# Splitting the second expert layer of a two-layer sparse block into three groups of tokens (4, 2 and 2 steps) instead of two (4 and 4)

## The chip, the cores and the metric

One Trainium2 chip, and of it one core. The metric is the device time of one execution in microseconds (us); lower is better. All data is float32, except where a routing count is made with bf16 ones and zeros. Engine names are those of the profile: PE is TensorE, DVE is VectorE, ACT is ScalarE, POOL is GpSimd, and SP is SyncE, which only issues DMAs here.

## The reference, cut to what matters

The input is x with shape (4, 1024, 128). Three residual sub-layers follow each other: an expert layer, an attention layer, and the same expert layer again with the same weights.

```python
def ffn(x):                       # x: (4, 1024, 128); 8 experts, hidden width 512
    xf = x.reshape(-1, 128)
    e = argmax(xf @ Wr.T + br)    # one expert for each token
    h = relu(xf @ W1[e].T + b1[e])
    return h @ W2[e].T + b2[e]    # the reference computes all 8 and picks one
x = x + 0.5 * ffn(layernorm(x))
x = x + attention(layernorm(x))   # linear attention, 16 heads, chunks of 128 tokens, with decay and a gate
x = x + 0.5 * ffn(layernorm(x))
```

## The kernel before

**Units, slots and tiles.** The 1024 positions of each of the 4 sequences are cut into 8 steps of 128, so a step holds 4 tiles of 128 tokens, one for each sequence. An expert layer does not run over steps. It sorts the tokens by expert and runs over slots, each of 128 places that all belong to one expert. A unit is a group of steps that are sorted together. For a unit of t tiles, t + 7 slots are always run, because each of the 8 experts can end in a slot that is not full. `SPLIT = ((3, 5), (4, 4))` makes two units in each layer: 12 tiles and 19 slots, 20 tiles and 27 slots in layer one; twice 16 tiles and 23 slots in layer two. Slots are numbered through by G: 0 to 45 are layer one, 46 to 68 are unit 2, and 69 to 91 are unit 3. In this text y(G) stands for the DVE instruction at line 820 that finishes slot G.

**What happens for a unit.** DVE takes the best expert of each token from the router's logits (`route_choose`), PE adds up the counts (`route_counts`), and DVE works out each token's place (`route_read_counts`, `route_count`, `route_place`) and the expert that owns each slot (`route_owners`). Then POOL sends each tile of 128 rows (576 bytes a row) to its places in a DRAM buffer `slots_in` by an indirect DMA, one for each tile (`sort_rows`, line 384). SP loads slots from there into a ring of 24 places in SBUF (`load_slot`, line 315) and the expert's W1 into a ring of 4 (`load_w1`, line 323).

**One slot.** DVE normalises the rows (line 798). PE transposes them (line 1034), ACT copies the result out of PSUM (line 499), PE does 8 matmuls with W1 (line 1042), ACT and DVE each take half of the relu (lines 514 and 813), PE does 8 matmuls with W2 (line 1052), and DVE adds the result to the row (line 820). That makes 17 matmul records for each slot. The slots are pipelined: in the loop's turn G, PE transposes slot G + 1, does the first product of G and the second of G - 1. POOL then scatters the finished rows to x1 or to the output by an indirect DMA, one for each slot (`scatter`, line 395). W1, b1 and b2 are addressed through registers that each engine loads from the owners' row.

**Order around the change.** Each engine's program is in order. Work of the attention layer's end and the routing of the last unit lie between the slots of layer two; a table `between` in each engine's `expert_pass(1, ...)` names the turn of each piece. POOL's order for layer two is: sort unit 2 in the attention layer's last part, scatter slots 46 to 51 (`EARLY_SCATTERS = 6`), sort unit 3, scatter all others. Before each scatter, and before each row sort of a unit that is not the first in its layer, POOL clears a piece of SBUF (`pause`, line 371), which puts a space between indirect DMAs. SP issues in its turn G the load of slot G + 6 and the W1 of slot G + 3. The load of a unit's first slot waits until the whole unit is sorted, and a load into a used ring place waits for the scatter of slot G - 24. POOL also takes a part of DVE's sums in the attention layer (`half_sum`, line 433); that is the same in both kernels.

Of the kernel before, what the change touches and what calls it, by code (L numbers as in the profile page):

```python
# [17 lines left out]
STEPS = SEQ // P  # L18
# [3 lines left out]

SPLIT = ((3, 5), (4, 4))
LAYERS, GROUPS = len(SPLIT), 2
UNITS = LAYERS * GROUPS
Unit = namedtuple("Unit", "layer first tiles slots start")
# [14 lines left out]
UNIT = list_units()  # L41
LAYER_TILES = UNIT[GROUPS].start
MAX_TILES = max(u.tiles for u in UNIT)
# [36 lines left out]
def step(k):  # L80
    return Step(k, k % 2)
# [20 lines left out]
def build(nc, x, w1t, bias, w2t, wrt, br, wqkv, wg1t, wg2, wo, gamma, beta, decay, const, out):  # L102
    with ExitStack() as ctx:
        def sb(name, shape, dt=F32):
            return ctx.enter_context(nc.sbuf_tensor(name, shape, dt))
# [73 lines left out]

        owner_ff = sb("owner_ff", [1, LAYER_TILES], I32)  # L180
        owner_d = sb("owner_d", [1, LAYER_TILES], I32)
        owner_fb = sb("owner_fb", [1, LAYER_TILES], I32)
        slot_of = [sb(f"slot_of{u}", [P, UNIT[u].tiles], I32) for u in range(UNITS)]

# [68 lines left out]
        ln_turn = lambda k: max(k + 1, 0)  # L253
        EARLY_SCATTERS = 6
        ROUTE_TURN = SPLIT[1][0] - 1 + 3

# [6 lines left out]
        wait_scattered = lambda eng, G: eng.wait_ge(scattered[G % SCATTER_SEMS], 16 * (G // SCATTER_SEMS + 1))  # L263
        layer_of = lambda G: G // LAYER_TILES
        unit_of = lambda G: max(u for u in range(UNITS) if UNIT[u].start <= G)
# [17 lines left out]
        def _(sp):  # L283
# [24 lines left out]
            def load_slot(G):  # L308
                u = unit_of(G)
                if first_of_unit(G):  # L310
                    sp.wait_ge(rows_sorted[u], 16 * UNIT[u].tiles)
                if G >= RING:
                    wait_scattered(sp, G - RING)
                at = (G - UNIT[u].start) * P
                sp.dma_start(in_ring(G), slots_in[u][at:at + P, :]).then_inc(slot_loaded[G % LOAD_SEMS], 16)

            def load_w1(G):
                if first_of_unit(G):
                    sp.wait_ge(owners_known[unit_of(G)], 1)
                k = G % LAYER_TILES  # L320
                e = sp.value_load(owner_ff[0:1, k:k + 1], min_val=0, max_val=(EXPERTS - 1) * FF)
                wait(sp, up_b, G - W1_BUFS + 1)
                sp.dma_start(w1_ring[G % W1_BUFS][:, :], w1t[:, bass.ds(e, FF)]).then_inc(w1_loaded[G % W1_BUFS], 16)
# [4 lines left out]
            SLOTS_AHEAD, W1_AHEAD, X1_AT = 6, 3, 36  # L328

            def loads(first, end, hooks):  # L330
                for G in range(first - SLOTS_AHEAD, end):
                    if G in hooks:
                        hooks[G]()
                    if G + SLOTS_AHEAD < end:
                        load_slot(G + SLOTS_AHEAD)
                    if first <= G + W1_AHEAD < end:
                        load_w1(G + W1_AHEAD)
# [6 lines left out]

            loads(0, LAYER_TILES, {X1_AT: first_group_back})
            for G in range(UNIT[1].start, LAYER_TILES):
                wait_scattered(sp, G)
            for c in range(SPLIT[0][0], STEPS):
                load_x1(c)
            fill_slots(2)  # L350
            fill_slots(3)
            loads(LAYER_TILES, LAYERS * LAYER_TILES, {})
            for G in range(LAYERS * LAYER_TILES - SCATTER_SEMS, LAYERS * LAYER_TILES):
                wait_scattered(sp, G)
# [3 lines left out]
        def _(pool):  # L358
# [15 lines left out]
            def sort_rows(u):  # L374
                unit = UNIT[u]
                pool.wait_ge(rows_kept, unit.layer * STEPS + (unit.first + unit.tiles) // BATCH)
                pool.wait_ge(fill_ready, 4)
                pool.wait_ge(ids_ready, 1 + 2 * min(u + 1, GROUPS))
                pool.wait_ge(slots_known[u], 1)
                pool.wait_ge(slots_filled[u], 16)  # L380
                for t in range(unit.tiles):
                    if u % GROUPS == 1:
                        pause()
                    pool.indirect_dma_start(  # L384
                        slots_in[u], bass.IndirectOffsetOnAxis(ap=slot_of[u][:, t:t + 1], axis=0),
                        row_of(unit.first + t), None).then_inc(rows_sorted[u], 16)
# [73 lines left out]
            sort_rows(1)  # L460
            scatter(0, LAYER_TILES)
            for b in range(BATCH):
# [3 lines left out]
            sort_rows(2)  # L466
            scatter(LAYER_TILES, LAYER_TILES + EARLY_SCATTERS)
            sort_rows(3)
            scatter(LAYER_TILES + EARLY_SCATTERS, LAYERS * LAYER_TILES)


        @block.scalar
        def _(act):
# [19 lines left out]
            def expert_pass(l, between):  # L493
                base, end = l * LAYER_TILES, (l + 1) * LAYER_TILES

# [137 lines left out]
            for k in TURNS:  # L633
# [3 lines left out]
                3: lambda: output_copy(8), 4: lambda: normalise_routed(8),  # L637
                6: lambda: route_copy(STEPS + 6, 0, bank[4]), 9: lambda: normalise_routed(9),
                11: lambda: route_copy(STEPS + 7, 1, bank[4])})


        @block.vector
        def _(dve):
# [130 lines left out]
            def route_owners(u):  # L774
                chain, slots = chains[u], UNIT[u].slots
                at = UNIT[u].start % LAYER_TILES
                part, owner_ = slice(at, at + slots), owner_f[:, 0:slots]
# [14 lines left out]
            def expert_pass(l, between):  # L792
                base, end = l * LAYER_TILES, (l + 1) * LAYER_TILES

# [179 lines left out]
            for k in TURNS:  # L974
# [5 lines left out]
                0: lambda: (output_stats(8), residual_stats(8), turn_small(8, 0, SMALL + 1, *both)),  # L980
                2: lambda: router_bias(5), 4: lambda: gate(step(7)), 5: lambda: residual_stats(9),
                6: lambda: (turn_small(9, 0, 6, ROUTED, ROUTED + BATCH), router_bias(6)),
                7: lambda: turn_small(9, 6, SMALL + 1, ROUTED, ROUTED + BATCH),
                11: lambda: (router_bias(7), route_choose(3)), 12: lambda: (route_read_counts(3), route_count(3)),
                13: lambda: route_place(3), 14: lambda: route_owners(3)})


        @block.tensor
        def _(pe):
# [32 lines left out]
            def expert_pass(l, between):  # L1022
                base, end = l * LAYER_TILES, (l + 1) * LAYER_TILES
                expert = {}
# [58 lines left out]
            def gate_product(s):  # L1083
                if s.n == 0:
                    pe.wait_ge(y_done, LAYER_TILES)
                wait(pe, delta_copied, s.n)
                mm(bank[6][:, :], wg_sb[:, :], xnT[s.par][:, :], start=True, stop=True).then_inc(gate_ready, 1)
# [116 lines left out]
            for k in TURNS:  # L1204
# [11 lines left out]
                2: lambda: out_transpose(step(7)), 4: lambda: (out_product(step(7)), route_transpose(step(6))),  # L1216
                5: lambda: route(6), 9: lambda: route_transpose(step(7)), 10: lambda: route(7),
                11: lambda: route_counts(3)})

# [61 lines left out]
```

## Time and profile before

| what | value |
|---|---|
| three runs | 505.95, 510.1 and 514.2 us; median 510.1 us |
| the profiled execution's own time | 506.26 us |
| its span, first to last instruction | 504.5 us |
| lies outside the span | 1.76 us |
| mean granted PE clock | 0.86 of full speed |
| y(46), the first slot of layer two finished | 366.40 us |
| y(91), the last slot finished | 497.02 us |

The span is the stretch that the trace covers, and positions in it are in us from its start. The runs lie within 1.6% of each other.

### The profile page before, as it was taken

How to read it: one execution, taken by the hardware profiler on the slowest of the kernel's cores; microseconds unless marked ns; L12 is line 12 of the kernel's file. 1: busy time of each engine (PE TensorE's matmuls, PEld its weight loads, DVE VectorE, ACT ScalarE, POOL GpSimd, SP SyncE). 2: the span in 40 equal slices, each digit the busy share in tenths (PEclk: the TensorE clock that was granted, in tenths of full speed). 3: DMA queues.
4: the chain of work that ended last, by engine and by line, in shares of the span. 5: the costliest groups of instructions: out<-in, count | busy, mean ns of one | idle time of the engine just before them, and what ended most of it. 6: DMA issues, size and time to landing. Idle time of an engine off the chain costs nothing.

```text
span 504.5 us, 10554 instructions
## 1 busy us (share of the span) xinstructions
PE 375.3 (74%) x2474; PEld 328.9 (65%) x2474; DVE 349.1 (69%) x1064; ACT 192.9 (38%) x590; POOL 302.4 (60%) x402
## 2 busy tenths in 40 slices
PE   4593049999999677976878869382699773499983
PEld 2592049999998456655656657362698563399983
DVE  3937006878777169999999999996777721167861
ACT  1360014555554413253562744402465211145541
POOL 1057885666665526778577676957051388856564
PEclk9655558999999879999999999677799975589998
DMA  8972425666674290000000000011554422356730
GB/s 246 282 308 83 147 80 153 196 200 199 200 238 125 67 298 15 0 2 0 2 1 1 0 1 1 0 36 59 157 155 144 119 75 78 106 149 195 206 116 6
DMA packets 54218, 56.08 MB, mean 111 GB/s; under 512 B 6828, under 2 KB 39881, under 8 KB 53904
## 3 DMA queue, kind: packets, MB, share of 16 engines
q1 hardware_dynamic: 48736, 45.85, 31.4%
q0 software_dynamic: 4992, 8.94, 4.9%
q10 hardware_dynamic: 432, 0.63, 0.4%
q8 instruction: 23, 0.38, 0.3%
q14 instruction: 35, 0.29, 0.2%
HBM read 39.69 MB, written 17.53 MB: 113 GB/s over the span
## 4 chain that ended last, share of the span: by engine, by line
PE 30%; DVE 22%; issue 20%; POOL 15%; another core or an unknown queue 6%; ACT 3%; DMA 1%; DVEq 1%; POOLq 1%; ACTq 0%
PE bank L1052 9%; PE bank L1042 8%; POOL out_x L395 7%; PE bank L1100 4%; POOL scratch L371 3%; DVE o_in L859 3%; POOL slots_in L384 3%; DVE st L646 2%; PE bank L1080 2%; PE bank L1006 2%; PE bank L1012 2%; PE bank L1134 2%; DVE tt L670 1%; DVE qS L850 1%
## 5 line engine op out<-in xcount | busy, mean ns | idle before, releaser
L1042 PE MATMUL bank<-slot_xT,w_ring 128*128 128x128 f32 x736 | 107.7, 290 | 20.1 <-issue 12.7
L1042 PEld LDWEIGHTS bank<-slot_xT,w_ring 128*128 128x128 f32 x736 | 96.3, 202 | 25.0 <-issue 20.8
L813 DVE TENSOR_SCALAR hT_b<-bank,b_cur 128x128 f32<-128x128 f32 x184 | 55.7, 344 | 49.8 <-remote 44.8
L384 POOL DMA_INDIRECT slots_in<-rows,slot_of x64 | 61.9, 967 | 47.1 <-DVE slot_of L772 32.8
L371 POOL MEMSET scratch<- 128x256 f32 x128 | 40.9, 320 | 64.8 <-DVE ring L820 35.5
L1100 PE MATMUL bank<-outer_all,decay_sb 128*128 128x256 f32 x256 | 70.5, 402 | 7.2 <-DVE outer_all L276 2.7
L1052 PE MATMUL bank<-w_sb,hT_a 128*128 x368 | 63.5, 298 | 12.4 <-issue 6.9
L514 ACT ACTIVATE hT_a<-bank,b_cur 128x128 f32<-128x128 f32 x184 | 57.3, 363 | 33.2 <-remote 18.1
L1100 PEld LDWEIGHTS bank<-outer_all,decay_sb 128*128 128x128 f32 x256 | 49.5, 203 | 24.4 <-issue 6.7
L276 POOL TENSOR_TENSOR outer_all<-qkv 128x512 f32<-128x512 f32 x60 | 63.6, 1084 | 2.6 <-ACT qkv L542 2.4
L1052 PEld LDWEIGHTS bank<-w_sb,hT_a 128*128 128x128 f32 x368 | 51.4, 202 | 17.2 <-issue 16.5
L1052 PE MATMUL bank<-w_sb,hT_b 128*128 x368 | 58.9, 285 | 0.0
L395 POOL DMA_INDIRECT x<-ring x46 | 44.6, 970 | 19.1 <-POOL scratch L371 18.7
L395 POOL DMA_INDIRECT out_x<-ring x46 | 44.9, 975 | 18.0 <-POOL scratch L371 13.7
L859 DVE TENSOR_REDUCE o_in<-qS 128x64 f32<-128x256 f32 (+1 forms) x64 | 53.5, 856 | 0.0
L820 DVE SCALAR_TENSOR_TENSOR ring<-bank,ring 128x128 f32<-128x128 f32 x92 | 26.7, 290 | 37.2 <-issue 14.2
L1052 PEld LDWEIGHTS bank<-w_sb,hT_b 128*128 128x128 f32 x368 | 51.4, 202 | 0.0
L850 DVE TENSOR_TENSOR qS<-bank,qkv 128x512 f32<-128x512 f32 x64 | 43.4, 679 | 11.5 <-PE bank L1100 7.2
L433 POOL TENSOR_TENSOR qS<-qS 128x256 f32<-128x256 f32 x28 | 20.3, 727 | 43.9 <-DVE qS L850 43.9
L507 ACT ACTIVATE b_cur<-b_t 128x4 f32 x92 | 18.9, 205 | 72.0 <-DVE hT_b L813 47.2
L798 DVE TENSOR_SCALAR slot_n<-ring 128x128 f32<-128x128 f32 x92 | 45.3, 494 | 1.2 <-DMA ring<-slots_in 0.9
L499 ACT ACTIVATE slot_xT<-bank 128x128 f32<-128x128 f32 x92 | 25.1, 273 | 46.9 <-remote 31.5
(117 smaller groups left out, 559.0 us busy)
## 6 DMA issues: line engine op xcount, KB each, us to landing
w_ring<-in_w1t SPq DMA_DIRECT2D x92, 256.0 KB
ring<-slots_in SPq DMA_DIRECT2D x92, 72.0 KB
slots_in<-fill SPq DMA_DIRECT2D x2, 1656.0 KB, 13.1
rows<-in_x SPq DMA_DIRECT2D x8, 256.0 KB, 6.4
w_sb<-in_w2t SPq DMA_DIRECT2D x1, 2048.0 KB
rows<-x SPq DMA_DIRECT2D x8, 256.0 KB, 5.0
slots_in<-fill SPq DMA_DIRECT2D x1, 1944.0 KB, 15.0
slots_in<-fill SPq DMA_DIRECT2D x1, 1368.0 KB, 8.7
```

Of the source, the lines that this page charges most:

```text
L276: return eng.tensor_tensor(u_.rearrange("p (h d e) -> p h d e", d=HD, e=HD), k_.rearrange("p (h d) e -> p h d e", d=HD), v_, ALU.mult)
L371: pool.memset(scratch[k % 2][:, :], 0.0).then_inc(paused, 1)
L384: pool.indirect_dma_start(slots_in[u], bass.IndirectOffsetOnAxis(ap=slot_of[u][:, t:t + 1], axis=0), row_of(unit.first + t), None).then_in ...
L395: pool.indirect_dma_start(x1 if layer_of(G) == 0 else out, bass.IndirectOffsetOnAxis(ap=ids_in_ring(G), axis=0), in_ring(G, 0, D), None, b ...
L514: last = nc.scalar.activation(hT_a[G % 2][:, f * P:(f + 1) * P], bank_a[:, f * P:(f + 1) * P], ACT.Relu, bias=b1_cur[G % 2][:, f:f + 1])
L798: nc.vector.tensor_scalar(slot_n[G % 3][:, :], in_ring(G, 0, D), in_ring(G, SCALE_AT, SCALE_AT + 1), in_ring(G, SHIFT_AT, SHIFT_AT + 1), A ...
L813: last = nc.vector.tensor_scalar(hT_b[G % 2][:, f * P:(f + 1) * P], bank_b[:, f * P:(f + 1) * P], b1_cur[G % 2][:, 2 + f:3 + f], 0.0, ALU. ...
L850: nc.vector.tensor_tensor(qS[h % 4][:, :].rearrange("p (b a e) -> p b a e", b=BATCH, e=HD), bank[h % 3][:, :].rearrange("p (b a e) -> p b ...
L859: nc.vector.tensor_reduce(o_in[:, h * w:(h + 1) * w].rearrange("p (a e) -> p a e", e=HD), qS[h % 4][:, :].rearrange("p (a d e) -> p a e d" ...
L1042: last = mm(to[:, f * P:(f + 1) * P], w1_ring[G % W1_BUFS][:, (2 * half + f) * P:(2 * half + f + 1) * P], slot_xT[G % 2][:, :], start=True ...
L1052: last = mm(y_bank[:, 0:D], h[:, f % 2 * P:(f % 2 + 1) * P], w2_sb[:, bass.ds(expert[G] + f * D, D)], start=(f == 0), stop=(f == FB - 1))
L1100: last = mm(to, decay_sb[:, (2 * h + a) * P:(2 * h + a + 1) * P], u, start=True, stop=True)
```

## The change

Layer two is sorted in three groups of 4, 2 and 2 steps. Unit 3 now has 8 tiles and 15 slots (69 to 83) and unit 4 has 8 tiles and 15 slots (84 to 98). POOL's order becomes: sort unit 2, 6 scatters, sort unit 3 (8 tiles), 18 scatters (52 to 69), sort unit 4 (8 tiles), the other scatters. The routing of unit 3 moves from turns 11 to 14 of the pass to turns 2 to 7; that of unit 4 lies in turns 13 to 17. The load of the first slots of a later unit is put off to 3 turns ahead of the unit instead of 6. Layer one and the attention code are as before.

```diff
-SPLIT = ((3, 5), (4, 4))
-LAYERS, GROUPS = len(SPLIT), 2
-UNITS = LAYERS * GROUPS
+SPLIT = ((3, 5), (4, 2, 2))
+LAYERS, GROUPS = len(SPLIT), len(SPLIT[0])
+UNITS = sum(len(s) for s in SPLIT)
...
-        EARLY_SCATTERS = 6
+        EARLY_SCATTERS = (6, 24)
...
+            def slot_due(H):
+
+                u = UNIT[unit_of(H)]
+                return H - SLOTS_AHEAD if u.first == 0 else max(H - SLOTS_AHEAD, u.start - W1_AHEAD)
...
-                    if G + SLOTS_AHEAD < end:
-                        load_slot(G + SLOTS_AHEAD)
+                    for H in range(first, end):
+                        if slot_due(H) == G:
+                            load_slot(H)
...
-            fill_slots(2)
-            fill_slots(3)
+            for u in range(GROUPS, UNITS):
+                fill_slots(u)
...
-                    if u % GROUPS == 1:
+                    if UNIT[u].first > 0:
                         pause()
...
             sort_rows(2)
-            scatter(LAYER_TILES, LAYER_TILES + EARLY_SCATTERS)
+            scatter(LAYER_START[1], LAYER_START[1] + EARLY_SCATTERS[0])
             sort_rows(3)
-            scatter(LAYER_TILES + EARLY_SCATTERS, LAYERS * LAYER_TILES)
+            scatter(LAYER_START[1] + EARLY_SCATTERS[0], LAYER_START[1] + EARLY_SCATTERS[1])
+            sort_rows(4)
+            scatter(LAYER_START[1] + EARLY_SCATTERS[1], LAYER_START[2])
...
-                6: lambda: route_copy(STEPS + 6, 0, bank[4]), 9: lambda: normalise_routed(9),
-                11: lambda: route_copy(STEPS + 7, 1, bank[4])})
+                6: lambda: route_copy(STEPS + 6, 0, bank[4]), 11: lambda: normalise_routed(9),
+                13: lambda: route_copy(STEPS + 7, 1, bank[4])})
...
-                2: lambda: router_bias(5), 4: lambda: gate(step(7)), 5: lambda: residual_stats(9),
-                6: lambda: (turn_small(9, 0, 6, ROUTED, ROUTED + BATCH), router_bias(6)),
-                7: lambda: turn_small(9, 6, SMALL + 1, ROUTED, ROUTED + BATCH),
-                11: lambda: (router_bias(7), route_choose(3)), 12: lambda: (route_read_counts(3), route_count(3)),
-                13: lambda: route_place(3), 14: lambda: route_owners(3)})
+                2: lambda: (router_bias(5), route_choose(3)), 4: lambda: (gate(step(7)), route_read_counts(3), route_count(3)),
+                5: lambda: residual_stats(9), 6: lambda: route_place(3),
+                7: lambda: route_owners(3), 8: lambda: (turn_small(9, 0, 6, ROUTED, ROUTED + BATCH), router_bias(6)),
+                9: lambda: turn_small(9, 6, SMALL + 1, ROUTED, ROUTED + BATCH),
+                13: lambda: (router_bias(7), route_choose(4)), 15: lambda: (route_read_counts(4), route_count(4)),
+                16: lambda: route_place(4), 17: lambda: route_owners(4)})
...
-                5: lambda: route(6), 9: lambda: route_transpose(step(7)), 10: lambda: route(7),
-                11: lambda: route_counts(3)})
+                5: lambda: route(6), 11: lambda: route_transpose(step(7)), 12: lambda: route(7),
+                3: lambda: route_counts(3), 14: lambda: route_counts(4)})
```

The other lines of the diff replace `LAYER_TILES` by the starts of the layers, since the two layers now have different numbers of slots (46 and 53).

## Rows read from the trace of the kernel before

**Rows 1.** The page, part 1: busy us (share of the span) xinstructions.
```profile
PE 375.3 (74%) x2474; PEld 328.9 (65%) x2474; DVE 349.1 (69%) x1064; ACT 192.9 (38%) x590; POOL 302.4 (60%) x402
```

**Rows 2.** The chain that ended last, 330 to 505 us, its shares by line.
```profile
by line: issue 22.0%; POOL out_x L395 20.9%; another core or an unknown queue 12.0%; POOL scratch L371 10.1%; POOL slots_in L384 8.8%; PE bank L1052 3.9%; PE bank L1042 3.4%; PE bank L1134 1.7%; DVEq L804 1.5%; DVE hT_b L813 1.0%; POOLq L86
```

**Rows 3.** Busy time by stretch in layer two; columns named in its first line.
```profile
core 0: us, PE busy (x) PEld busy (x) DVE busy (x) ACT busy (x) POOL busy (x), PEclk, DMA share, GB/s
...
399.00:412.00 13.00, 9.15 (x54) 7.83 (x54) 6.12 (x24) 3.08 (x13) 11.30 (x18) 0.85 0.32 103
412.00:423.00 11.00, 6.79 (x30) 5.41 (x29) 2.37 (x8) 1.38 (x5) 9.68 (x17) 0.66 0.14 50
423.00:433.00 10.00, 2.56 (x9) 1.85 (x8) 0.61 (x2) 0.83 (x3) 8.96 (x14) 0.50 0.48 143
...
463.00:479.00 16.00, 16.00 (x144) 15.97 (x143) 12.78 (x44) 9.35 (x34) 9.53 (x15) 1.00 0.72 209
```

**Rows 4.** Timeline of DVE, line 820: start, us, and idle before; y(55), y(58) to y(64).
```profile
388.33 0.29 DVE L820 SCALAR_TENSOR_TENSOR ring<-bank,ring 128x128 f32<-128x128 f32 x1 [0.28 <-PE bank L1052]
...
399.86 0.28 DVE L820 SCALAR_TENSOR_TENSOR ring<-bank,ring 128x128 f32<-128x128 f32 x1
...
402.71 0.28 DVE L820 SCALAR_TENSOR_TENSOR ring<-bank,ring 128x128 f32<-128x128 f32 x1
...
407.71 0.29 DVE L820 SCALAR_TENSOR_TENSOR ring<-bank,ring 128x128 f32<-128x128 f32 x1 [1.65 <-remote]
...
412.20 0.29 DVE L820 SCALAR_TENSOR_TENSOR ring<-bank,ring 128x128 f32<-128x128 f32 x1 [0.94 <-remote]
...
420.30 0.29 DVE L820 SCALAR_TENSOR_TENSOR ring<-bank,ring 128x128 f32<-128x128 f32 x1 [2.36 <-remote]
...
433.47 0.29 DVE L820 SCALAR_TENSOR_TENSOR ring<-bank,ring 128x128 f32<-128x128 f32 x1 [5.26 <-remote]
...
440.81 0.29 DVE L820 SCALAR_TENSOR_TENSOR ring<-bank,ring 128x128 f32<-128x128 f32 x1 [0.92 <-remote]
```

**Rows 5.** The same timeline later: y(66) and y(91).
```profile
446.51 0.29 DVE L820 SCALAR_TENSOR_TENSOR ring<-bank,ring 128x128 f32<-128x128 f32 x1 [0.44 <-PE bank L1052]
...
497.02 0.29 DVE L820 SCALAR_TENSOR_TENSOR ring<-bank,ring 128x128 f32<-128x128 f32 x1 [1.43 <-PE bank L1052]
```

**Rows 6.** Timeline of POOL: scatter(51), unit 3's first and last sort, scatter(63).
```profile
379.94 0.97 POOL L395 DMA_INDIRECT out_x<-ring  x1 [0.43 <-issue]
398.86 0.31 POOL L371 MEMSET scratch<- 128x256 f32 x1 [17.95 <-DVE slot_of L772]
399.54 0.97 POOL L384 DMA_INDIRECT slots_in<-rows,slot_of  x1 [0.38 <-issue]
...
421.40 0.96 POOL L384 DMA_INDIRECT slots_in<-rows,slot_of  x1 [0.17 <-issue]
...
438.97 0.97 POOL L395 DMA_INDIRECT out_x<-ring  x1 [0.17 <-issue]
```

**Rows 7.** Timeline of SP: W1 of slots 62 and 65, then slot 69.
```profile
393.65 0.34 SPq L323 DMA_DIRECT2D w_ring<-in_w1t  x1
...
405.56 0.34 SPq L323 DMA_DIRECT2D w_ring<-in_w1t  x1
423.71 0.32 SPq L315 DMA_DIRECT2D ring<-slots_in  x1
```

**Rows 8.** Timeline of layer one's start: slot 0 transposed by PE and copied by ACT.
```profile
48.37 0.47 PE L1034 MATMUL bank<-const_sb,slot_n 128*128 128x128 f32 x1 [0.35 <-issue]
...
65.64 0.28 ACT L499 ACTIVATE slot_xT<-bank 128x128 f32<-128x128 f32 x1 [20.88 <-remote]
```

**Rows 9.** Busy time by stretch while unit 2 is sorted (332.2 to 352.1 us).
```profile
332.00:344.00 12.00, 9.30 (x43) 7.05 (x41) 11.90 (x37) 1.09 (x2) 9.08 (x10) 0.96 0.16 56
344.00:350.00 6.00, 0.00 (x0) 0.00 (x0) 1.66 (x4) 0.00 (x0) 4.47 (x6) 0.72 0.15 51
```

**Rows 10.** Timeline of DVE: a routing operation on 128 and a small one on 4 elements.
```profile
379.84 0.16 DVE L677 SCALAR_TENSOR_TENSOR uu<-tt,var 128x4 f32<-128x4 f32 x1
...
390.44 0.29 DVE L739 TENSOR_REDUCE best<-place 128x16 f32<-128x128 f32 x1
```

More of the change, by code:

```diff
@@ L41 @@
 UNIT = list_units()
-LAYER_TILES = UNIT[GROUPS].start
+LAYER_START = [next(u.start for u in UNIT if u.layer == l) for l in range(LAYERS)] + [UNIT[-1].start + UNIT[-1].slots]
+LAYER_SLOTS = max(b - a for a, b in zip(LAYER_START, LAYER_START[1:]))
 MAX_TILES = max(u.tiles for u in UNIT)
@@ L177, in build @@
         owner_f = sb("owner_f", [1, MAX_SLOTS])
-        owner_ff = sb("owner_ff", [1, LAYER_TILES], I32)
-        owner_d = sb("owner_d", [1, LAYER_TILES], I32)
-        owner_fb = sb("owner_fb", [1, LAYER_TILES], I32)
+        owner_ff = sb("owner_ff", [1, LAYER_SLOTS], I32)
+        owner_d = sb("owner_d", [1, LAYER_SLOTS], I32)
+        owner_fb = sb("owner_fb", [1, LAYER_SLOTS], I32)
         slot_of = [sb(f"slot_of{u}", [P, UNIT[u].tiles], I32) for u in range(UNITS)]
@@ L263, in build @@
         wait_scattered = lambda eng, G: eng.wait_ge(scattered[G % SCATTER_SEMS], 16 * (G // SCATTER_SEMS + 1))
-        layer_of = lambda G: G // LAYER_TILES
+        layer_of = lambda G: max(l for l in range(LAYERS) if LAYER_START[l] <= G)
         unit_of = lambda G: max(u for u in range(UNITS) if UNIT[u].start <= G)
@@ L319, in load_w1 @@
                     sp.wait_ge(owners_known[unit_of(G)], 1)
-                k = G % LAYER_TILES
+                k = G - LAYER_START[layer_of(G)]
                 e = sp.value_load(owner_ff[0:1, k:k + 1], min_val=0, max_val=(EXPERTS - 1) * FF)
@@ L343, in first_group_back @@
                     load_x1(c)
-            loads(0, LAYER_TILES, {X1_AT: first_group_back})
-            for G in range(UNIT[1].start, LAYER_TILES):
+            loads(0, LAYER_START[1], {X1_AT: first_group_back})
+            for G in range(UNIT[1].start, LAYER_START[1]):
                 wait_scattered(sp, G)
@@ L349, in _ @@
                 load_x1(c)
-            fill_slots(2)
-            fill_slots(3)
-            loads(LAYER_TILES, LAYERS * LAYER_TILES, {})
-            for G in range(LAYERS * LAYER_TILES - SCATTER_SEMS, LAYERS * LAYER_TILES):
+            for u in range(GROUPS, UNITS):
+                fill_slots(u)
+            loads(LAYER_START[1], LAYER_START[2], {})
+            for G in range(LAYER_START[2] - SCATTER_SEMS, LAYER_START[2]):
                 wait_scattered(sp, G)
@@ L460, in _ @@
             sort_rows(1)
-            scatter(0, LAYER_TILES)
+            scatter(0, LAYER_START[1])
             for b in range(BATCH):
@@ L493, in expert_pass @@
             def expert_pass(l, between):
-                base, end = l * LAYER_TILES, (l + 1) * LAYER_TILES
+                base, end = LAYER_START[l], LAYER_START[l + 1]
                 def copy_xT(G):
@@ L775, in route_owners @@
                 chain, slots = chains[u], UNIT[u].slots
-                at = UNIT[u].start % LAYER_TILES
+                at = UNIT[u].start - LAYER_START[UNIT[u].layer]
                 part, owner_ = slice(at, at + slots), owner_f[:, 0:slots]
@@ L792, in expert_pass @@
             def expert_pass(l, between):
-                base, end = l * LAYER_TILES, (l + 1) * LAYER_TILES
+                base, end = LAYER_START[l], LAYER_START[l + 1]
                 def normalise_slot(G):
@@ L1022, in expert_pass @@
             def expert_pass(l, between):
-                base, end = l * LAYER_TILES, (l + 1) * LAYER_TILES
+                base, end = LAYER_START[l], LAYER_START[l + 1]
                 expert = {}
@@ L1084, in gate_product @@
                 if s.n == 0:
-                    pe.wait_ge(y_done, LAYER_TILES)
+                    pe.wait_ge(y_done, LAYER_START[1])
                 wait(pe, delta_copied, s.n)
```

## The prediction, made before the changed kernel was run

> **What bounds the kernel now.** The page's first part gives no engine more than 74% of the span [rows 1], so no engine's speed sets the whole, and the stage of the change has to be read by itself. The chain of waits for the last 175 us leads through POOL: scatters 20.9%, the clears before them 10.1%, row sorts 8.8% [rows 2]. A chain that runs along an engine that is merely busy beside the others proves little, so I went on to the busy times by stretch. From 463 to 479 us PE is busy for all of 16.00 us, with 144 matmul records [rows 3]. At 17 a slot that is 8.5 slots, or 1.9 us a slot: this is the free pace, and PE sets it. From 399 to 433 us every engine but POOL is mostly idle: PE is busy 9.15 of 13, 6.79 of 11 and then 2.56 of 10 us, and its granted clock falls to 0.85, 0.66 and 0.50, half speed, after it had thinned out [rows 3]. That is the hole in layer two.
>
> Its size: y(58) comes at 399.86 and y(66) at 446.51 [rows 4, 5], 8 slots in 46.65 us where 8 x 1.9 = 15.2 would do, so 31.4 us are lost. POOL's timeline runs over the same stretch: idle for 17.95 us until unit 3's places are known, then 16 sorts from 399.54 to 421.40 (15 spacings, 1.46 us each), and without a gap 12 late scatters, slots 52 to 63, to 438.97 [rows 6]. I call such a run of 28 indirect DMAs at 1.46 us a dense spell. y(64) comes only 1.84 us after the last of them [rows 4, 6], and the pace is back at once. In the spell the slots come later and later: the intervals from y(58) to y(64) are 2.85, 5.0, 4.5, 8.1, 13.2 and 7.3 us [rows 4].
>
> There are two readings. One: dense POOL DMAs hold up the signals between the other engines. Two: SP's queue is blocked, since it waits at slot 69's load from 405.56 to 423.71 for the sort, with W1 of slot 66 behind it [rows 7]. For the second, the times agree roughly. Against it: W1 of slot 62 was issued at 393.65 and that of slot 65 at 405.56 [rows 7], yet y(62) came at 420.30 and y(63) at 433.47 [rows 4], with nothing of theirs in the blocked queue. For the first, layer one has a purer case: under 20 sorts PE began slot 0's transpose at 48.37 (0.47 us), and ACT, which had only to copy it, began at 65.64 [rows 8], 17 us later. I take the first.
>
> **The change part by part.** The sum is made on the profiled execution, 504.5 us of span and 1.76 outside it, 506.26 in all; that is 3.8 us below the median of 510.1. I add the same difference to the median.
>
> *Seven more slots.* Layer two has 53 slots instead of 46, whatever the data: 7 x 1.9 = 13.3 us, all on PE's path [rows 3]. Nothing covers them; each also needs a W1 load and a scatter, which fit beside 1.9 us as they do for the others.
>
> *Routing twice.* Now `route_choose`, the counts and `route_place` lie in three turns, y(55) to y(58): 11.53 us for 3 slots [rows 4], 5.8 over pace. (The owners' turn falls into the spell and is counted there.) The new units have 64 wide elements instead of 128. An operation takes 0.29 us at 128 and 0.16 at 4 [rows 10], so some 0.22 at 64 (between them on a line); some 14 wide operations in a routing save 1.0 us. Two routings cost 2 x 4.85 = 9.7: 3.9 more. They stand in DVE's order ahead of the relu, so nothing hides them.
>
> *The long spell goes:* -31.4 us.
>
> *Two short spells come.* POOL no longer idles before the sort, because unit 3's places are known by turn 6, when scatter(51) goes out. The sort is 8 x 1.46 = 11.7 us. I lay the slots over it as they came in the old spell, which has the same start: at +1.0, +3.9, +8.9 and +13.3 us from the sort's start [rows 4, 6]. So three scatters are late when it ends, the fourth falls due while they are sent, and the spell ends after 12 DMAs, 17.5 us. The next slot then comes at about +19 instead of at +21.4. That makes 4 slots in 18.0 us against 7.6: 10.4 us. The second sort, after scatter(69), finds the same: 20.8 in all. Bounds: from below nothing, since while unit 2 was sorted DVE was busy for 11.90 of the first 12 us with 10 sorts issued; from above a standstill, as in the 6 us after them, where PE did nothing [rows 9], and in layer one [rows 8]. In a standstill hardly any scatter falls late: 10 DMAs, 14.6 us, and 1.9 us for the two slow slots after it (y(64) to y(66), 5.7 us against 3.8 [rows 4, 5]), so 33 us for both. I take 20.8 because the old spell lies in the same loop with the same loads, and its first third is exactly this piece.
>
> *Moves with one answer, at nothing.* The scatters of the old order are kept, and POOL's queue has no idle of its own while slots wait. `route_counts(3)` in PE's turn 3 waits for DVE's turn 2, but the product behind it needs that turn's relu anyway. The fill of a third buffer (7 slots x 72 KB more) is issued long before, behind the attention layer. A gain below nothing is possible for SP: its wait moves behind W1 of slot 68, and the sort is over by then (about 395 us). In its place comes a shorter lead: the first load of a unit is issued when PE is through with slot 64 (79), and DVE wants it some 2.5 turns later, 4.7 us; as a row for such a load there is only the general pace. From nothing to 5 us for both units; I take nothing, as the ring's other loads are never waited for at pace.
>
> Sum: 13.3 + 3.9 - 31.4 + 20.8 = +6.6. Span 511.1, own time 512.9; on the median 510.1 + 6.6 = 516.7 us.
>
> **The rivals.** *Standstill:* each short spell stops everything, as in layer one. 13.3 + 3.9 - 31.4 + 33 = +18.8: 529 us, slower. It decides from 12.3 us a spell on, where the whole passes 2%. For it: layer one's 17 us [rows 8], and W1 loads run all through the new spells, while from 405.56 to 423.71 SP issued none [rows 7]; the two worst intervals came with and after the loads' return. Against it: the old spell's own first 12 us.
>
> *Short spells are nearly covered:* signals grow late only with the spell's length, 12 us are free as for unit 2 [rows 9], and each costs one late hand-over or two, 3 us. 17.2 - 31.4 + 6 = -8.2: 502 us. Against it: y(60) was 3 us late within 9 us [rows 4].
>
> *It was SP's queue:* the hole came from the blocked loads, the new order waits nowhere, and dense spells are free. 17.2 - 31.4 = -14.2: 496 us, faster. The rows against it stand above. The Trainium skill speaks for this case: "SBUF — State Buffer", section "Who interferes with whom", says that only the port pair that VectorE and GpSimd share causes contention, and that "PE and ACT never wait on anyone". By that rule POOL's sorts could not hold PE or ACT, and the change would come out at this rival's 496 us. The trace speaks against it, if the 17 us between PE's end and ACT's start in layer one [rows 8] are no port's matter but a late signal, which the page does not treat.
>
> *Late first loads* at the two unit borders, 5 us on top of the forecast: 522 us.
>
> **How the numbers follow.** A measurement of this kernel can tell about 2% from no change, that is 10.2 us: below 499.9 is faster, above 520.3 slower. The forecast's own case, 512 to 522 us, has 0.47; the standstill 0.25; covered spells 0.14; SP's queue 0.09; late loads 0.05. Faster is SP's queue with a share of the covered case, 0.12. Slower is the standstill without its mildest form, the late loads and the top of the forecast's case, 0.36. Within 2% remains, 0.52. The range reaches over the covered case and to the standstill, 501 to 529, and leaves out SP's queue and the worst of the standstill.
>
> **What would show it.** In the new profile: y(46) to the last y should take 137 us (130.6 before), with 53 of them; two spells of some 12 indirect DMAs at 1.46 us, from about 383 us and some 45 us later; in each 4 slots take 16 to 20 us, and PE's clock dips briefly or not at all; three turns over pace in each routing, 4.85 us; free pace 1.9 us. If a spell has fewer than 3 slots, the standstill holds; if it has 6 or more, one of the two fast rivals. The sum is wrong if the late signals depend on something other than the spell, such as loads that run beside it, since I scaled by length alone; and it is wrong in the other direction if late signals of the first spell last into the paced part, where POOL sends a DMA every 1.9 us.

## The result, and the profile after

The changed kernel takes 520.83 us in the median of 4 runs (519.99 to 522.66), the kernel before 508.02 in 4. The ratio is 1.0267, with a 95% interval from 1.0216 to 1.0318: slower by 12.8 us, just beyond the 2% that the prediction treats as no change. Here and below a median is over all executions of a kernel, while a ratio leaves out the few executions that were disturbed as a whole, so it is not exactly the quotient of two medians. The profiled execution has a span of 518.2 us and a time of 519.99.

The page, part 1, of the changed kernel, which answers to [rows 1]:

```profile
PE 392.1 (76%) x2595; PEld 345.4 (67%) x2595; DVE 363.2 (70%) x1124; ACT 200.8 (39%) x618; POOL 311.2 (60%) x416
```

PE has 121 records more: 7 slots of 17 are 119. The chain of waits from 340 us on leads through POOL again. The stretch isn't the one of [rows 2], which begins at 330 us, but the shares of POOL's scatters and sorts are clearly larger now:

```profile
by line: issue 39.7%; POOL out_x L403 27.3%; POOL slots_in L392 14.7%; POOL scratch L379 12.0%; POOLq L88 1.2%; POOLq L403 0.8%; POOLq L105 0.7%; POOLq L388 0.0%; POOLq L387 0.0%
```

The timeline of DVE, line 830 (line 820 of before), shows the slots: y(46), y(52) to y(56), then y(70) to y(75), and y(98). It answers to [rows 4, 5].

```profile
368.67 0.29 DVE L830 SCALAR_TENSOR_TENSOR ring<-bank,ring 128x128 f32<-128x128 f32 x1 [0.69 <-PE bank L1063]
...
387.47 0.28 DVE L830 SCALAR_TENSOR_TENSOR ring<-bank,ring 128x128 f32<-128x128 f32 x1
...
393.89 0.29 DVE L830 SCALAR_TENSOR_TENSOR ring<-bank,ring 128x128 f32<-128x128 f32 x1 [2.40 <-remote]
...
399.88 0.29 DVE L830 SCALAR_TENSOR_TENSOR ring<-bank,ring 128x128 f32<-128x128 f32 x1 [1.65 <-remote]
...
403.67 0.29 DVE L830 SCALAR_TENSOR_TENSOR ring<-bank,ring 128x128 f32<-128x128 f32 x1 [0.19 <-remote]
...
407.37 0.29 DVE L830 SCALAR_TENSOR_TENSOR ring<-bank,ring 128x128 f32<-128x128 f32 x1 [1.10 <-PE bank L1063]
...
441.16 0.29 DVE L830 SCALAR_TENSOR_TENSOR ring<-bank,ring 128x128 f32<-128x128 f32 x1 [0.24 <-issue]
...
446.09 0.29 DVE L830 SCALAR_TENSOR_TENSOR ring<-bank,ring 128x128 f32<-128x128 f32 x1 [3.19 <-remote]
...
452.10 0.29 DVE L830 SCALAR_TENSOR_TENSOR ring<-bank,ring 128x128 f32<-128x128 f32 x1 [2.40 <-remote]
...
458.78 0.29 DVE L830 SCALAR_TENSOR_TENSOR ring<-bank,ring 128x128 f32<-128x128 f32 x1 [1.65 <-remote]
...
461.42 0.29 DVE L830 SCALAR_TENSOR_TENSOR ring<-bank,ring 128x128 f32<-128x128 f32 x1 [1.00 <-PE bank L1063]
...
464.02 0.29 DVE L830 SCALAR_TENSOR_TENSOR ring<-bank,ring 128x128 f32<-128x128 f32 x1 [0.28 <-PE bank L1063]
...
510.18 0.29 DVE L830 SCALAR_TENSOR_TENSOR ring<-bank,ring 128x128 f32<-128x128 f32 x1 [1.43 <-PE bank L1063]
```

Layer two, from the first finished slot to the last, takes 141.5 us; before it took 130.6 [rows 5, and the table of the times]. In place of one hole there are two, 19.9 us for 4 slots and 20.3 us for 4. In both, DVE waits for something whose sender the trace doesn't name ("remote"). What y(53) needed from PE was the second product of slot 53, and PE had ended it at 389.62 us:

```profile
388.47 0.71 PE L1063 MATMUL bank<-w_sb,hT_a 128*128 x4
...
389.01 0.61 PE L1063 MATMUL bank<-w_sb,hT_b 128*128 x4
```

DVE was free from 391.49 us on, and yet y(53) began only at 393.89. This is what "a late signal" means below: the work is done, and the engine that waits for it starts some microseconds later. POOL's timeline (line 392 is a sort, 403 a scatter) has the sorts of unit 3 from 387.22 to 397.41 and of unit 4 from 442.39 on, each after a scatter and at 1.46 us. Three late scatters follow each group of 8 sorts at the same spacing, to 401.81 and 456.99, so a spell is 11 indirect DMAs. These rows answer to [rows 6]:

```profile
385.76 0.97 POOL L403 DMA_INDIRECT out_x<-ring  x1 [0.43 <-POOL scratch L379]
386.73 0.33 POOL L379 MEMSET scratch<- 128x256 f32 x1
387.22 0.96 POOL L392 DMA_INDIRECT slots_in<-rows,slot_of  x1 [0.17 <-issue]
...
397.41 0.96 POOL L392 DMA_INDIRECT slots_in<-rows,slot_of  x1 [0.17 <-POOL scratch L379]
...
401.81 0.97 POOL L403 DMA_INDIRECT out_x<-ring  x1 [0.17 <-issue]
...
442.39 0.96 POOL L392 DMA_INDIRECT slots_in<-rows,slot_of  x1 [0.17 <-issue]
```

The busy times of the two holes answer to [rows 3]. Each PEclk is a mean over its stretch, so 0.72 and 0.65 hide that the clock is at its lower level, half speed, for a part of it. The third row is of a view of its own, cut to such a part, and shows 0.50.

```profile
392.00:398.00 6.00, 3.39 (x16) 2.91 (x14) 2.10 (x11) 0.90 (x3) 5.34 (x9) 0.72 0.33 104
...
447.00:454.00 7.00, 4.29 (x22) 3.80 (x22) 1.67 (x6) 1.57 (x7) 6.21 (x10) 0.65 0.29 92
...
401.60:407.60 6.00, 4.35 (x21) 4.05 (x20) 2.48 (x9) 3.31 (x13) 2.30 (x4) 0.50 0.39 112
```

Read in this way, PE runs at half speed in four parts of the two holes (around 396, 404, 452 and 461 us), each after it had thinned out; in the kernel before it is at 0.50 from 408.5 to 414.5 and from 418.8 to 445.3 us. PE is still at 0.50 from 459.6 to 462.2 us, when POOL no longer sends at 1.46 us, and the two slots around it, y(74) and y(75), take 2.6 us each in place of 1.9. A spell's cost below includes such slots.

### The profile page after: what moved, and what is told of

Read it like the earlier page. It is cut to its first block, busy times and chain, and to the rows that moved or that the text cites. A ratio compares the mean times of both kernels' runs of the same rounds, so it can differ in the third digit from the quotient of the medians.

```text
span 518.2 us, 11134 instructions
## 1 busy us (share of the span) xinstructions
PE 392.1 (76%) x2595; PEld 345.4 (67%) x2595; DVE 363.2 (70%) x1124; ACT 200.8 (39%) x618; POOL 311.2 (60%) x416
## 4 chain that ended last, share of the span: by engine, by line
issue 27%; PE 22%; POOL 19%; DVE 17%; another core or an unknown queue 5%; SPq 4%; ACT 1%; POOLq 1%; DVEq 1%; DMA 0%; ACTq 0%
POOL out_x L403 9%; PE bank L1063 8%; PE bank L1053 7%; POOL slots_in L392 6%; POOL scratch L379 4%; DVE o_in L869 4%; PE bank L1111 3%; PE bank L1145 2%; PE bank L1091 2%; SPq L289 1%; SPq L299 1%; DVE qS L860 1%; DVE st L656 1%; DVE tt L680 1%
## 5 line engine op out<-in xcount | busy, mean ns | idle before, releaser
L1053 PE MATMUL bank<-slot_xT,w_ring 128*128 128x128 f32 x792 | 116.2, 289 | 17.6 <-DVE hT_b L823 8.2
L1053 PEld LDWEIGHTS bank<-slot_xT,w_ring 128*128 128x128 f32 x792 | 104.3, 203 | 22.6 <-issue 11.8
L823 DVE TENSOR_SCALAR hT_b<-bank,b_cur 128x128 f32<-128x128 f32 x198 | 59.9, 344 | 41.1 <-remote 35.4
L1063 PE MATMUL bank<-w_sb,hT_a 128*128 x396 | 67.1, 294 | 13.1 <-issue 7.9
L524 ACT ACTIVATE hT_a<-bank,b_cur 128x128 f32<-128x128 f32 x198 | 61.7, 363 | 27.6 <-PE bank L1053 16.4
L1063 PEld LDWEIGHTS bank<-w_sb,hT_a 128*128 128x128 f32 x396 | 54.4, 199 | 18.0 <-issue 17.6
L403 POOL DMA_INDIRECT out_x<-ring x53 | 51.5, 972 | 23.2 <-POOL scratch L379 20.0
L1063 PE MATMUL bank<-w_sb,hT_b 128*128 x396 | 63.2, 284 | 0.0
L1063 PEld LDWEIGHTS bank<-w_sb,hT_b 128*128 128x128 f32 x396 | 54.9, 201 | 0.0
L517 ACT ACTIVATE b_cur<-b_t 128x4 f32 x99 | 20.3, 205 | 82.5 <-DVE hT_b L823 65.8
L808 DVE TENSOR_SCALAR slot_n<-ring 128x128 f32<-128x128 f32 x99 | 50.2, 508 | 0.7 <-DMA ring<-slots_in 0.6
L441 POOL TENSOR_TENSOR qS<-qS 128x256 f32<-128x256 f32 x28 | 20.4, 728 | 46.4 <-DVE qS L860 46.4
L509 ACT ACTIVATE slot_xT<-bank 128x128 f32<-128x128 f32 x99 | 27.0, 273 | 44.8 <-remote 24.9
## 6 DMA issues: line engine op xcount, KB each, us to landing
slots_in<-fill SPq DMA_DIRECT2D x2, 1080.0 KB, 12.7
```

The costliest lines, as they stand in the source:

```text
L403: pool.indirect_dma_start(x1 if layer_of(G) == 0 else out, bass.IndirectOffsetOnAxis(ap=ids_in_ring(G), axis=0), in_ring(G, 0, D), None, b ...
L524: last = nc.scalar.activation(hT_a[G % 2][:, f * P:(f + 1) * P], bank_a[:, f * P:(f + 1) * P], ACT.Relu, bias=b1_cur[G % 2][:, f:f + 1])
L808: nc.vector.tensor_scalar(slot_n[G % 3][:, :], in_ring(G, 0, D), in_ring(G, SCALE_AT, SCALE_AT + 1), in_ring(G, SHIFT_AT, SHIFT_AT + 1), A ...
L823: last = nc.vector.tensor_scalar(hT_b[G % 2][:, f * P:(f + 1) * P], bank_b[:, f * P:(f + 1) * P], b1_cur[G % 2][:, 2 + f:3 + f], 0.0, ALU. ...
L1053: last = mm(to[:, f * P:(f + 1) * P], w1_ring[G % W1_BUFS][:, (2 * half + f) * P:(2 * half + f + 1) * P], slot_xT[G % 2][:, :], start=True ...
L1063: last = mm(y_bank[:, 0:D], h[:, f % 2 * P:(f % 2 + 1) * P], w2_sb[:, bass.ds(expert[G] + f * D, D)], start=(f == 0), stop=(f == FB - 1))
```

## The experiments

"Layer two" below is the time from y(46) to the last y in the profiled execution; it is free of the scatter of what lies ahead of it: y(46) came anywhere from 364.2 to 369.2 us in the 14 profiled executions, changed and unchanged alike. Ratios are to the kernel before, run on the same chip.

**Is it SP's blocked queue?** The kernel before with SP's order of the changed kernel alone:

```diff
-                    if G + SLOTS_AHEAD < end:
-                        load_slot(G + SLOTS_AHEAD)
+                    for H in range(first, end):
+                        if G == (max(H - SLOTS_AHEAD, UNIT[3].start - W1_AHEAD) if H >= UNIT[3].start else H - SLOTS_AHEAD):
+                            load_slot(H)
```

> The kernel before (groups of 4 and 4), with one edit of SP's order: the loads of unit 3's first slots are put off from 6 to 3 turns ahead, as in the changed kernel, so that W1 of slots 66 to 68 no longer stands behind the wait for the sort. Theory (dense POOL DMAs make the other engines' signals late): nothing changes, within 3 us of before, and the intervals from y(58) to y(64) stay at 3 to 13 us. Rival (the hole is SP's blocked queue): 25 to 31 us faster, and the hole is gone.

Measured: 504.55 us, ratio 0.9992 (0.9946 to 1.0038): no change. Its profiled execution took 510.17 us, so only its pattern is read: from y(59) on, the seven slots to y(66) came at 5.2 to 6.6 us each. The blocked queue was not what limited the kernel before. But the pattern did change: without it the intervals no longer grow to 13.2 us. It will come back below.

**Is it POOL's order?** `EARLY_SCATTERS = 13` instead of 6 in the kernel before.

> The kernel before, with EARLY_SCATTERS 13 in place of 6: POOL scatters slots 52 to 58 while it waits for unit 3's places, and sorts then. Theory: 7 late scatters leave the spell, which becomes 16 sorts and about 5 scatters, 21 DMAs and 31 us instead of 28 and 41; the loss of 31 us shrinks to about 24, so 7 us faster (3 to 12). Rival (only the sort itself, or SP's wait for its end, counts): the sort starts and ends at the same time, so no change.

Measured: 497.07 us, ratio 0.9846 (0.9761 to 0.9931), layer two 121.2 us. A one-number edit makes the kernel before faster, by 0.7 to 2.4%, and so is better than both kernels; whether it passes 2% is open. The late scatters count, not only the sorts.

**What do the spells cost in all?** Both kernels without their later sorts:

```diff
-                if first_of_unit(G):
+                if first_of_unit(G) and u <= 2:
                     sp.wait_ge(rows_sorted[u], 16 * UNIT[u].tiles)
...
-                sp.dma_start(in_ring(G), slots_in[u][at:at + P, :])
+                sp.dma_start(in_ring(G), slots_in[min(u, 2)][at:at + P, :])
...
             def sort_rows(u):
+                if u > 2:
+                    return
```

> The kernel before without the 16 row sorts of unit 3: its slots are loaded from unit 2's sorted rows, so the output lacks unit 3's tokens, while all loads, products and scatters stay. It measures what the long spell costs in all. Theory and rival alike: about 31 us faster than before. If it is under 20, the hole has another cause than the sorts and what follows them.

> The changed kernel (4, 2 and 2) without the row sorts of units 3 and 4, whose slots are loaded from unit 2's sorted rows; the output lacks their tokens. The change without its spells: theory says 25 us faster than the changed kernel (the two spells cost 12.5 us each by its trace), which is 12 us faster than before and 17 to 19 us slower than the kernel before without its sorts (7 slots at 1.9 us and a second routing). If the difference between the two kernels without sorts is far from 17, the slots or the routing were mis-sized and not the spells.

Measured: 480.52 us (ratio 0.9528, 0.9462 to 0.9594) and 493.67 us (ratio 0.9778, 0.9659 to 0.9897). Layer two takes 99.5 us without sorts in groups of 4 and 4, and 116.6 in groups of 4, 2 and 2. So the spells cost 130.6 - 99.5 = 31.1 us before and 141.5 - 116.6 = 24.9 after, and slots and routing 17.1 us. The whole of the first kernel gained only 24.5, less than layer two did: its last 11.2 us behind y(91), against 7.5 before, took 3.7 of it back, and y(46) came 1.5 us later. For the same reasons the two kernels without sorts differ by only 13.2 us as wholes, where 17 to 19 was expected; the 17.1 us are layer two's alone.

**Is it POOL's time or its DMAs?** In the kernel without sorts, each sort of units 3 and 4 becomes two more clears:

```diff
                     if UNIT[u].first > 0:
                         pause()
+                    if u > 2:
+                        pause()
+                        pause()
+                        continue
```

> The changed kernel without the row sorts of units 3 and 4 (their slots are loaded from unit 2's sorted rows, the output lacks their tokens), but with POOL kept busy in each sort's place by two more clears, some 1.5 us a tile. It parts POOL's time from its DMAs. Theory (indirect DMAs in close order make the other engines' signals late): as without sorts, 120 to 123 us from y(46) to the last y against 116.6 without sorts and 141.5 in the changed kernel, the rest for the late scatters sent in close order; the whole at 494 to 500 us. Rival (what counts is that POOL is busy and scatters fall late): as the changed kernel, 520 us.

Measured: 505.29 us, ratio 0.9969 (0.9918 to 1.0020), layer two 130.4 us. Neither expectation was met, and the trace says why. The 24 clears took 6.4 us, where 8 sorts take 11.7, so they matched the sorts' time on POOL only in part. Its timeline, 24 clears and that of the next scatter in one run on POOL:

```profile
383.74 6.41 POOL L379 MEMSET scratch<- 128x256 f32 x25
```

and DVE (line 812 is the normalising of a slot) and PE beside it:

```profile
384.69 5.54 DVE L812 TENSOR_SCALAR slot_n<-ring 128x128 f32<-128x128 f32 x1
...
385.49 0.71 PE L1067 MATMUL bank<-w_sb,hT_a 128*128 x4
...
386.03 0.61 PE L1067 MATMUL bank<-w_sb,hT_b 128*128 x4
...
390.29 0.48 PE L1049 MATMUL bank<-const_sb,slot_n 128*128 128x128 f32 x1 [3.64 <-DVE slot_n L812]
```

One DVE instruction that takes 0.34 to 0.54 us elsewhere takes 5.54, as long as the clears follow each other, and PE then waits for it by name. The second run of clears holds the same instruction for 6.44 us. These two stops (8.1 us for y(53) where the kernel without sorts takes 3.1, 8.5 for y(72) where it takes 1.9) are 11.6 of the 13.8 us over the kernel without sorts. It is another stop than that of the spells, in which DVE's instructions keep their length and their waits are "remote". The control brought a fault of its own. Whether signals stay prompt while POOL is busy without DMAs it can't show: PE's products at 385.49 and 386.03 came in order, but they lie in the first 3 us of the clears, and in the changed kernel the products in the first 3 us of the sorts did so too. POOL's time is parted from its spacing by the kernels with two clears, below. The Trainium skill, "SBUF — State Buffer", section "Who interferes with whom", says that VectorE in a mode with two ports and GpSimd exclude each other for a whole instruction. The trace fits this for the stop of 5.54 us, though it doesn't show DVE's mode; it adds that back-to-back clears keep DVE out for all of the run.

**Does the spacing matter?** The changed kernel with no clear ahead of each sort of units 3 and 4 (`if unit.layer == 0 and UNIT[u].first > 0: pause()`), and with two.

> The changed kernel without the clear ahead of each sort of units 3 and 4, so that the sorts go out every 1.26 us instead of every 1.46. Theory with closeness as the measure: denser is worse, each spell costs 13 to 18 us instead of 12.5, the whole is the same or up to 10 us slower. Rival (each sort costs the time POOL takes for it, however spaced: 25 us for 16 sorts is 1.56 us a sort): 16 x 0.2 = 3 us faster.

> The changed kernel with two clears ahead of each sort of units 3 and 4, one sort every 1.95 us, about the pace at which scatters do no harm. Theory with closeness as the measure: the sorts themselves do no harm, only the 6 or 7 late scatters after them at 1.46 us do; each spell costs 4 to 8 us instead of 12.5, the whole 8 to 15 us faster than the changed kernel. Rival (a sort costs POOL's time for it): 16 x 0.5 = 8 us slower.

Measured: 523.1 us (ratio 1.0322, 1.0222 to 1.0421; layer two 144.6) and 511.73 us (ratio 1.0092, 1.0042 to 1.0142; layer two 135.7). Without clears the sorts are 1.26 us apart and over 1.6 us sooner, and nothing is gained; y(53) alone takes 12.7 us. With two clears the sorts leave 1.71 us apart, less than the 1.95 I had reckoned, and do no harm that shows: y(53) to y(57) take what they do without sorts, to 0.3 us. The harm comes when they are over and the late scatters follow at 1.46:

```profile
396.07 0.96 POOL L394 DMA_INDIRECT slots_in<-rows,slot_of  x1 [0.17 <-POOL scratch L379]
397.04 0.33 POOL L379 MEMSET scratch<- 128x256 f32 x1
397.53 0.98 POOL L405 DMA_INDIRECT out_x<-ring  x1 [0.17 <-issue]
```

and DVE (line 832), y(55) to y(58) of that kernel:

```profile
392.60 0.29 DVE L832 SCALAR_TENSOR_TENSOR ring<-bank,ring 128x128 f32<-128x128 f32 x1 [0.77 <-PE bank L1065]
394.49 0.29 DVE L832 SCALAR_TENSOR_TENSOR ring<-bank,ring 128x128 f32<-128x128 f32 x1 [0.24 <-PE bank L1065]
396.83 0.29 DVE L832 SCALAR_TENSOR_TENSOR ring<-bank,ring 128x128 f32<-128x128 f32 x1 [0.28 <-issue]
405.75 0.29 DVE L832 SCALAR_TENSOR_TENSOR ring<-bank,ring 128x128 f32<-128x128 f32 x1 [1.67 <-remote]
```

1.89 us a slot in the middle of the sorts, 8.9 us once the scatters close up (4.0 in the kernel without sorts). Six scatters at 1.46 us, from 397.53 to 404.86, were enough for this. The reading that a sort costs POOL's time for it, however spaced, falls: POOL works through the two clears and the sorts with gaps of 0.17 us at most, as busy as ever, and no slot is late.

**Do the loads beside it matter?** W1 loads of the changed kernel cut to 64 of 512 columns after the first 4 slots of layer two.

> The changed kernel with the W1 loads of layer two cut to 64 of 512 columns after the first 4 slots (the output is of mixed weights), so that SP's loads move an eighth of W1's bytes beside the spells. Theory (POOL's DMAs alone): each spell still costs 11 to 13 us and the whole is within 5 us of the changed kernel. Rival (a spell does harm only together with the loads' traffic): the spells cost under 6 us each and the whole is 12 us or more faster.

Measured: 518.61 us, ratio 1.0246 (1.0153 to 1.0340), layer two 141.1 us, and y(53) to y(55) at 6.4, 6.0 and 3.8 us as in the changed kernel. The two spells, y(52) to y(57) and y(70) to y(75), take 20.4 and 22.8 us, against 22.7 and 22.9 in the changed kernel. So an eighth of W1's bytes does much the same harm. The loads of the slots themselves (72 KB each) were left as they were, so this speaks of W1's traffic alone.

**Spacing everywhere.** The changed kernel, and the kernel before with 13 early scatters, with two clears, or one of 384 columns, ahead of each later sort and each scatter of layer two:

```diff
                         wait_scattered(pool, G - SCATTER_SEMS)
                     pause()
+                    if layer_of(G) == 1:
+                        pause()
```

> The changed kernel with two clears ahead of every sort of units 3 and 4 and of every scatter of layer two, so that POOL can never send indirect DMAs closer than 1.71 us. Theory (it is the spacing of 1.46 us that makes signals late, 1.71 does not): no late stretch anywhere, 117 to 120 us from y(46) to the last y, as without sorts; but POOL's own sum (69 DMAs x 1.71 = 118 us and some 8 us of waiting) then ends last, so the whole is 497 to 503 us. Rival (a late scatter does harm at any spacing): the intervals after each sort stay at 5 to 9 us and the whole is 512 us or more.

> The changed kernel with one clear of 384 instead of 256 columns ahead of every sort of units 3 and 4 and every scatter of layer two: a spacing of about 1.57 us, between the harmful 1.46 and the harmless 1.71. If harm sets in below 1.57: 491 to 497 us, POOL's queue is shorter than with two clears. If it sets in above it: late stretches of 5 us and more return, and the whole is 505 to 518 us.

> The kernel before (4 and 4) with 13 early scatters and two clears ahead of each sort of unit 3 and each scatter of layer two. Theory: no late stretch; instead slot 69 is wanted some 20 us after y(59) while 16 sorts take 27 us, so one wait of 7 to 10 us for the sort stands at y(69); 108 to 112 us from y(46) to y(91), the whole at 484 to 490 us, faster than with 13 early scatters alone (497). Rival (spacing doesn't matter, each sort costs its time on POOL): 27 us lost, 500 us.

> As the last one, with one clear of 384 columns (about 1.57 us of spacing) in place of two. If 1.57 us is harmless the sort is over 2 us sooner and the whole is 482 to 488 us; if it is harmful, intervals of 4 to 8 us as with 13 early scatters alone, and 492 to 498 us.

Measured, against the kernel before at 504.8 us:

| kernel | spacing on POOL, us | time, us | ratio (95%) | layer two, us |
|---|---|---|---|---|
| 4, 2, 2, two clears | 1.71 | 501.16 | 0.9968 (0.9890 to 1.0045) | 117.0 |
| 4, 2, 2, one wide clear | 1.57 | 505.61 | 1.0064 (0.9988 to 1.0141) | 128.5 |
| 4, 4, early 13, two clears | 1.71 | 496.26 | 0.9875 (0.9804 to 0.9946) | 121.8 |
| 4, 4, early 13, one wide clear | 1.57 | 495.03 | 0.9851 (0.9767 to 0.9936) | 122.5 |

With two clears the changed kernel runs layer two in 117.0 us, what it takes without any sorts (116.6). All 16 sorts then cost nothing that shows there. The spell's first slots, y(53) to y(56), line 834:

```profile
388.68 0.28 DVE L834 SCALAR_TENSOR_TENSOR ring<-bank,ring 128x128 f32<-128x128 f32 x1
391.64 0.28 DVE L834 SCALAR_TENSOR_TENSOR ring<-bank,ring 128x128 f32<-128x128 f32 x1
393.82 0.29 DVE L834 SCALAR_TENSOR_TENSOR ring<-bank,ring 128x128 f32<-128x128 f32 x1 [0.68 <-PE bank L1067]
395.71 0.29 DVE L834 SCALAR_TENSOR_TENSOR ring<-bank,ring 128x128 f32<-128x128 f32 x1 [0.24 <-PE bank L1067]
```

But the last y is at 483.71 and the span 500.6: POOL still sends scatters every 1.71 us, the last at 493.68. Of 24.5 us gained in layer two, 9 go to this tail, and as a whole the kernel is no faster than the one before (0.9968, 0.9890 to 1.0045). At 1.57 us the harm is about halved and not gone: layer two takes 128.5 us, 11.9 over the kernel without sorts where 1.46 us cost 24.9, and slots that run at 1.9 to 2.3 us there took up to 3.6 us.

In the kernel with groups of 4 and 4 the spacing removed the late signals too (at 1.57 us not quite), but brought out the limit that stood behind them, so that it gained nothing over 13 early scatters alone (0.9846). With two clears the pace from y(60) to y(64) is 1.9 to 2.2 us, and then one interval is 25.5 us. PE and SP (W1 of slot 65, slot 69, W1 of slot 66):

```profile
433.98 2.04 PE L1046 MATMUL bank<-slot_xT,w_ring 128*128 128x128 f32 x8 [22.14 <-issue]
```

```profile
402.98 0.34 SPq L323 DMA_DIRECT2D w_ring<-in_w1t  x1
429.96 0.32 SPq L315 DMA_DIRECT2D ring<-slots_in  x1
431.02 0.34 SPq L323 DMA_DIRECT2D w_ring<-in_w1t  x1
```

W1 of slot 66 stands behind slot 69's wait for the sort, and DVE finishes slot 65 only behind slot 66's relu in its order. I had expected the wait at y(69) and 7 to 10 us; it came at y(65) and cost 23.6 us over the pace. This is the rival of SP's queue, now real. The kernel that goes on from here, with 13 early scatters, a spacing of 1.57 to 1.71 us and SP's later loads together, was not run.

## Why the prediction held, and where it was too low

The time lies in the range, 501 to 529, and 4.1 us above the forecast of 516.7. Of the three outcomes, "slower" came, which had 0.36, and not "within 2%", which had 0.52. Measured against the kernel before it is +12.8 us where +6.6 was forecast, so the change was nearly twice the forecast. Only 4.1 us of that show in the time, because the forecast stood on a median of 510.1 us from three runs, and the fourth moved it to 508.02. The mechanism and its terms, one by one, in layer two:

- **Seven slots and the second routing, 13.3 + 3.9 = 17.2.** The two kernels without sorts differ by 17.1 us. Right; with 52 and 45 intervals at the pace of 1.9 us, 3.8 of them are left for routing.
- **The long spell, -31.4.** Without sorts, 31.1 us go. Right.
- **Two short spells, 20.8.** By the kernels without sorts, 24.9: this term was mis-sized by 4.1 us, and it is nearly all that is missing of +10.9 in layer two. The step that was mis-sized is the laying of the old spell's slots over the new ones, "4 slots in 18.0 us against 7.6": 4 slots took 19.9 and 20.3 us, although each spell was one DMA shorter than the forecast's 12. The old spell began with an interval of 2.85 us, the new ones with 6.4 and 4.9. With the slow fifth slot, the first spell, y(52) to y(57), took 22.7 us against 12.5 without sorts, 10.2 us. The second, y(70) to y(75), took 22.9 against 9.5, 13.4 us. In the kernel without sorts (line 832) these four times are:

```profile
384.48 0.28 DVE L832 SCALAR_TENSOR_TENSOR ring<-bank,ring 128x128 f32<-128x128 f32 x1
...
397.00 0.29 DVE L832 SCALAR_TENSOR_TENSOR ring<-bank,ring 128x128 f32<-128x128 f32 x1 [0.28 <-issue]
...
428.76 0.29 DVE L832 SCALAR_TENSOR_TENSOR ring<-bank,ring 128x128 f32<-128x128 f32 x1 [0.24 <-issue]
...
438.24 0.29 DVE L832 SCALAR_TENSOR_TENSOR ring<-bank,ring 128x128 f32<-128x128 f32 x1 [0.25 <-issue]
```

That the first spell's 10.2 agrees with the forecast's 10.4 is luck. Its slots were 1.9 us slower than forecast, but the turns it is laid over (DVE's small work, 3.0 to 3.1 us for y(53) and y(54) without sorts) take 10.2 us for 4 slots and not 7.6, so some lateness is hidden. The second spell lies over slots at the free pace, where all of it shows, and there "finds the same" fails as a cost. This explanation is read from the intervals and was not tried by itself. The remaining 1.3 us are the sum of small differences elsewhere; y(84) alone took 3.6 us, 1.7 more than without sorts.

- **Where the spells lie.** They were to start at about 383 us and some 45 us later; they started at 387.2 and 442.4, 55 us later. The forecast gave the 18 slots between them the free pace and one spell, 44.6 us. But DVE's small work and its routing slow y(58) to y(63) to 2.2 to 3.9 us, in the kernel without sorts as well. PE's clock was to dip briefly or not at all; it fell to half speed four times, as above.
- **The moves at nothing, SP's shorter lead.** At y(69) and y(84) of the kernel without sorts the intervals are 2.0 and 1.9 us. Right; the rival of late first loads falls. (In the changed kernel y(84) took 3.6 us, but so did it in the kernel before, 3.7, where 84 isn't the first slot of a unit.)
- **Rivals.** Standstill is out: 4 slots came in each spell. Its cost was nearer than it looks, though: the prediction saw 2% passed from 12.3 us a spell on, and the mean of the two is 12.5. Nearly covered is out. SP's queue is out as the cause of the old hole (ratio 0.9992), though it was the next limit.
- **The rest.** 2.3 us of the profiled execution's 13.7 lie before y(46), where nothing was changed. The same point varies by 5 us among executions.

The bet was also that lateness grows with the length of a spell. It holds only roughly: both short spells reached 6 us a slot with their first or second slot, and in the kernel before, once SP's queue was free, the intervals stayed between 5.2 and 6.6 us. The measure that the runs bear out is the spacing of POOL's DMAs.

## What to carry to other kernels

Before splitting work to break up a stall, price the stall's cause: here the split shortened the close run of DMAs and paid 17 us in new slots and a second routing for 6 us of gain, while changing how many scatters go ahead of the sort (6 to 13) gained 8 us, and spacing the DMAs freed layer two of the split kernel of the sorts' cost altogether, though not the kernel as a whole. Count what a queue has to send against the slowest harmless pace: 69 DMAs at 1.71 us are 118 us, as long as the loop itself, so at this spacing a further gain would need fewer of them, which no run here tried. And when a wait is taken away, look at once for the one behind it in another engine's order; SP's blocked queue cost nothing that shows until the signals were prompt.

## What the runs showed of the hardware

In layer two of this kernel, indirect DMAs that leave POOL every 1.46 us make signals between the other engines late, whether they carry rows to be sorted or finished rows. It shows soon: y(53) was late within 7 us of the first sort, and six scatters over 7.3 us (397.53 to 404.86) were enough for an interval of 8.9 us. At 1.57 us layer two still loses 11.9 us of the 24.9, at 1.71 us nothing that shows (117.0 against 116.6). That POOL is busy is not enough, since at 1.71 us it is as busy. Cutting W1's loads to an eighth of their bytes changes little (layer two 141.1 against 141.5 us). The spacing alone doesn't set how much is lost, however: in layer one, where the kernel before also sends a sort every 1.46 us, from 46 us on, ACT started 17 us late [rows 8], and in layer two of the same kernel a slot took 4 to 13 us. Which part of the chip holds the signals back, no run here tells.

25 clears on POOL in close order hold a DVE instruction that reads and writes SBUF for as long as they last, 5.54 and 6.44 us. PE went on beside them at 385.49 and 386.03, until it needed that instruction's result.
